# Score tile ahead of the max tile in the first pair of each attention slot, on TensorE's queue

## The chip, the cores and the metric

The kernel runs on one core of a Trainium2 chip (trn2). The metric is the device time of one execution in microseconds (us). Engines are called PE (TensorE), PEld (its weight loads), DVE (VectorE), ACT (ScalarE), POOL (GpSimd) and SP (SyncE, which here only issues DMAs).

## The reference

The input is x, 8 sequences of 1024 tokens with 256 features. Three blocks follow one another:

```python
x = x + 0.5 * ffn(layernorm(x))      # top-2 gated expert + shared projection
x = x + attention(layernorm(x))      # 16 heads of 16 dims, causal
x = x + 0.5 * ffn(layernorm(x))
```

The change is in the attention:

```python
q = q / math.sqrt(D)
scores = jnp.einsum('bhqd,bhkd->bhqk', q, k)
scores = jnp.where(causal, scores, -inf)
attn = jax.nn.softmax(scores, axis=-1)
out = jnp.einsum('bhqk,bhkd->bhqd', attn, v)
```

The softmax subtracts each query's maximum over its keys before the exponential.

## The kernel before

There are three stages, one after the other: `stage_a` (first feed-forward block and the projections to q, k and v, in 16 chunks of 512 tokens), `stage_b` (attention) and `stage_c` (output projection and second feed-forward block). Each engine's program is written out by hand, in order, with semaphores between the engines; there is no scheduler.

`stage_b` works through 32 groups of four heads (8 sequences x 16 heads). The scores of a group are computed twice.

- The first time ("max tiles") only the row maxima are wanted. `max_tile` (L1157) gives PE a tile of one PSUM bank (queries on the partitions, up to 512 keys along the bank; one matmul or two), and two tiles make a unit. DVE reads a unit out of a pair of banks (`maximum`, L1094; `dve_unit`, L435): one custom instruction for each of one or two reductions, each with a read of the accumulator into `pm`. The last read of a unit raises `m_read`. There are two pairs of banks, so the first tile of a unit waits until DVE has read the unit two before it (L1162). There are 36 max tiles, 18 units, to a group.
- The second time ("score tiles") the scores come transposed, keys on the partitions. `score_tile` (L1165) multiplies k with q; two more rows of the operands carry the maximum, negated, so that it is subtracted by the matmul. ACT takes the exponential of the tile into `b_probs` (L1079). Score tiles have three PSUM banks in a ring, so a tile waits until ACT has read the tile three before it (`p_ready`, L1182). POOL zeroes the blocks above the diagonal.

A group's score tiles are divided into nine slots of four heads (`SLOTS`; the causal triangle is packed in rows of 512 columns, so that a slot's tile is one matmul of 512 columns in slots 0 and 3 to 7, and two matmuls in slot 1 (384 + 128), 2 (256 + 256) and 8 (384 + 128)). After the third tile of each slot comes the value step of two slots before (`values`, L1188; col-tiled matmuls of `b_probs` with v). So PE goes through nine slots of four pairs each, a pair being a max tile of one or two groups ahead and a score tile of this group. The order in which this stands on PE's queue is the loop at L1224 to L1231, and nothing else sets it. The first group's maxima are computed ahead, and the last group has no max tiles between its score tiles.

The max tile of the first pair has an odd number in its group, so it completes a unit: it is the one that DVE waits for. The max tile of the second pair opens the next unit and waits for DVE. The third completes, the fourth opens.

Which half of the operands' rows a head has depends on its number (`head_rows`): even heads lie from row 0, odd ones from row 64. The heads of the score tiles are taken in the order 1, 0, 2, 3 (`S_ORDER`), and the max tiles beside them have the other half each time.

Once a group, in slot 6 after the value step, PE transposes the negated maxima of the next group (`turn_m`, L1154), ACT copies them (L1058), and a DMA puts them into the rows of q for the score tiles of that group, from slot 0 on.

Of the kernel before, what the change touches and what calls it, by code (L numbers as in the profile page):

```python
# [116 lines left out]
def head_rows(h, n):  # L117

    return slice(h % 2 * HALF, h % 2 * HALF + n)
# [741 lines left out]
def stage_b(nc, psum, pairs_of_banks, const, scratch, ahead, chunk):  # L861
    ident, _, zero, *_, hold = const
    with ExitStack() as ctx:
# [65 lines left out]
        def score_bank(g, t, last):  # L929

            if last:
                n = t % (SB + MB)
                return m_bank[n - SB] if n >= SB else s_bank[ring(g, n) % SB]
            return s_bank[ring(g, t) % SB]

        def turn_bank(g):

            return s_bank[(ring(g, TURN_TILE) - 1) % SB]

        def groups(eng, step):  # L940

            step(Group(0, 0), False)
            with loop(eng, 0, (NG - 2) // NBUF) as r:
                for k in range(1, NBUF + 1):
                    step(Group(r, k), False)
            step(Group(0, NG - 1), True)
# [196 lines left out]
        @block.tensor  # L1143
        def _(pe):
            def turn_m(g):

                pe.wait_ge(m_chain, g.at(2, 2))
                if g.k or not isinstance(g.r, int):
                    p = g.next(-1)
                    pe.wait_ge(p_ready, p.at(TILES, TURN_TILE - SB + 1))  # L1150
                    bank = turn_bank(p)
                else:
                    bank = s_bank[SB - 1]
                pe.transpose(bank[:, 0:P],  # L1154
                             mparts[:].rearrange("p q r n -> p (q r n)").bitcast(F32), ident[:]).then_inc(m_turned, 1)

            def max_tile(g, t):  # L1157
                u = t // 2
                if t == 0:
                    pe.wait_ge(stacked[g.buf], g.turn(STACK, STACK))  # L1160
                if t % 2 == 0 and not (g.first and u < 2):
                    pe.wait_ge(m_read, g.at(NUNIT, u - 1))  # L1162
                ahead.pe_unit_tile(pe, qs[g.buf], ks[g.buf], u, t % 2, m_bank[t % MB])

            def score_tile(g, s, n, last):  # L1165
                t, h = s * GH + n, S_ORDER[n]
                if t == 0:
                    if g.first:
                        pe.wait_ge(ones_placed, 16 * 2 * NBUF)
                    pe.wait_ge(m_placed[g.buf], g.turn(32, 32))  # L1170
                if last and t >= SB:
                    if t == SB:
                        pe.wait_ge(m_read, NG * NUNIT + UNITS_AHEAD)
                    if t >= SB + MB:
                        pe.wait_ge(p_ready, g.at(TILES, t - SB - MB + 1))
                elif not last and TURN_TILE <= t < TURN_TILE + SB:
                    if t == TURN_TILE + SB - 1:
                        pe.wait_ge(m_out, g.at(1, 2))
                    else:
                        pe.wait_ge(p_ready, g.at(TILES, t - SB + 2))  # L1180
                elif not (g.first and t < SB):
                    pe.wait_ge(p_ready, g.at(TILES, t - SB + 1))  # L1182
                for j, q0, w, off in SLOTS[s]:
                    done = pe.matmul(score_bank(g, t, last)[:, off:off + w], ks[g.buf][head_rows(h, SROWS_M), h // 2, j * P:(j + 1) * P],  # L1184
                                     qs[g.buf][head_rows(h, SROWS_M), h // 2, q0:q0 + w], start=True, stop=True)
                done.then_inc(s_tile, 1)

            def values(g, s):  # L1188

                pe.wait_ge(p_ready, g.at(TILES, GH * (s + 1)))  # L1190
                if DIAG[s]:
                    pe.wait_ge(p_masked, g.at(ND, DIAG_SLOTS.index(s) + 1))
                if s == 0:
                    pe.wait_ge(vx_ready, g.at(1, 1))
                    if not g.first:
                        pe.wait_ge(o_out, g.at(2))
                if s == LOW_DONE + 1:
                    pe.wait_ge(o_out, g.at(2, 1))
                pieces = VALUE_PIECES[s]
                for n, (src, j, q0, w, off) in enumerate(pieces):  # L1200
                    col = q0 % BANK
                    for h in range(GH):
                        last = pe.matmul(o_bank[2 * D * h:2 * D * (h + 1), col:col + w], vx[g.buf][:, j, h, :],  # L1203
                                         probs[:, PROB_BUF[src], h, off:off + w], start=(j == 0),
                                         stop=(s in (LOW_DONE, HIGH_DONE) and n == len(pieces) - 1),
                                         tile_position=(0, 2 * D * h))
                last.then_inc(pv_done, 1)

            def event(g, s):
                if s >= 2:  # L1210
                    values(g, s - 2)
                elif not g.first:
                    values(g.next(-1), NSLOT - 2 + s)

            def step(g, last):
                def maxima(s, n):
                    if not last:
                        t = (s + AHEAD) * GH + n + 1
                        if t < TILES:
                            max_tile(g.next(1), t)  # L1220
                        else:
                            max_tile(g.next(2), t - TILES)

                for s in range(NSLOT):  # L1224
                    for n in range(GH):
                        maxima(s, n)
                        score_tile(g, s, n, last)
                        if n == GH - 2:
                            event(g, s)
                            if s == TURN_SLOT and not last:  # L1230
                                turn_m(g.next(1))  # L1231

            for t in range(2 * UNITS_IN_A, TILES):
                max_tile(Group(0, 0), t)
            for t in range(AHEAD * GH + 1):
                max_tile(Group(0, 1), t)
                if t == GH - 1:
                    turn_m(Group(0, 0))
            groups(pe, step)
            for s in (NSLOT - 2, NSLOT - 1):  # L1240
                values(Group(0, NG - 1), s)
# [453 lines left out]
```

## Time and profile before

| what | value |
|---|---|
| median of 3 runs | 1322.26 us (1321.27 to 1323.11) |
| the profiled execution, its own time | 1320.54 us |
| its span, first to last instruction | 1318.7 us |
| PE matmul busy, share of the span | 1225.8 us, 93% |
| PE weight loads | 801.9 us, 61% |
| DVE | 1105.0 us, 84% |
| ACT | 921.7 us, 70% |
| POOL | 434.7 us, 33% |
| granted clock of TensorE, mean | 0.971 |
| DVE, the reductions of the max tiles (L435), 1036 of them | 727.1 us, mean 753 ns |
| ACT, the exponentials (L1079), 1152 of them | 598.6 us, mean 609 ns |

The busy time of an engine is the union of its instructions' times; PE's matmuls are pipelined and their ends are modelled, so a busy PE needn't be at its peak. In the page's picture of the span in 40 slices, slices 12 to 33 (the attention) have PE, DVE and the granted clock at 9 tenths or more throughout.

### The profile page before, as it was taken

How to read it: one execution, taken by the hardware profiler on the slowest of the kernel's cores; microseconds unless marked ns; L12 is line 12 of the kernel's file. 1: busy time of each engine (PE TensorE's matmuls, PEld its weight loads, DVE VectorE, ACT ScalarE, POOL GpSimd, SP SyncE). 2: the span in 40 equal slices, each digit the busy share in tenths (PEclk: the TensorE clock that was granted, in tenths of full speed). 3: DMA queues.
4: the chain of work that ended last, by engine and by line, in shares of the span. 5: the costliest groups of instructions: out<-in, count | busy, mean ns of one | idle time of the engine just before them, and what ended most of it. 6: DMA issues, size and time to landing. Idle time of an engine off the chain costs nothing. (4 is left out here: it accounts for less than half of the span.)

```text
span 1318.7 us, 35998 instructions
## 1 busy us (share of the span) xinstructions
PE 1225.8 (93%) x9331; PEld 801.9 (61%) x9331; DVE 1105.0 (84%) x3904; ACT 921.7 (70%) x1858; POOL 434.7 (33%) x843
## 2 busy tenths in 40 slices
PE   3999999997999999999999999999999996799996
PEld 3988888875544444444444444444444442799996
DVE  4788888868999999999999999999999994567775
ACT  3666666641777887887887887887887887356663
POOL 3333333301222222222322322322222222577771
PEclk9999999997899999999999999999999999799998
DMA  3356655893464654664664644654654643556641
GB/s 116 129 222 223 223 223 223 244 266 100 72 108 83 107 102 82 108 101 82 108 101 82 113 96 85 109 96 86 109 96 89 112 89 111 192 171 197 203 149 65
DMA packets 121853, 173.74 MB, mean 132 GB/s; under 512 B 44012, under 2 KB 71788, under 8 KB 121804
## 3 DMA queue, kind: packets, MB, share of 16 engines
q1 hardware_dynamic: 121816, 173.30, 54.4%
q8 instruction: 17, 0.28, 0.1%
q14 instruction: 20, 0.16, 0.0%
HBM read 96.08 MB, written 76.02 MB: 131 GB/s over the span
## 5 line engine op out<-in xcount | busy, mean ns | idle before, releaser
L435 DVE CUSTOM_DVE_ANT_0 junk<-banks,mask 128x768 bf16<-128x768 f32 (+7 forms) x1036 | 727.1, 753 | 6.0 <-issue 5.7
L1079 ACT ACTIVATE b_probs<-banks 128x512 f32<-128x512 f32 x1152 | 598.6, 609 | 135.6 <-PE banks L1184 131.3
L428 PE MATMUL banks<-ks,qs 48*128 48x512 f32 (+3 forms) x1056 | 295.5, 386 | 24.4 <-DVE pm L435 15.7
L1203 PE MATMUL banks<-b_probs,b_vx 128*32 128x512 f32 (+3 forms) x3072 | 308.2, 496 | 4.3 <-POOL b_probs L1039 2.0
L1184 PE MATMUL banks<-qs,ks 50*128 50x512 f32 (+3 forms) x1056 | 309.2, 389 | 0.8 <-ACT b_probs L1079 0.4
L428 PEld LDWEIGHTS banks<-ks,qs 48*128 48x128 f32 x1056 | 168.9, 191 | 184.3 <-DVE pm L435 153.6
L165 POOL TENSOR_TENSOR hold_pool<-zero 128x1 f32<-128x1 f32 x192 | 37.2, 194 | 592.6 <-ACT b_probs L1079 463.5
L1184 PEld LDWEIGHTS banks<-qs,ks 50*128 50x128 f32 x1056 | 164.9, 187 | 21.5 <-ACT b_probs L1079 18.4
L1039 POOL TENSOR_SCALAR_AFFINE_SELECT b_probs<-b_probs 128x512 f32<-128x512 f32 x256 | 158.3, 636 | 0.0
L428 PE MATMUL banks<-b_ks,b_qs 48*128 48x512 f32 (+2 forms) x499 | 135.9, 376 | 7.6 <-DVE pm L435 6.2
L1184 PE MATMUL banks<-b_qs,b_ks 50*128 50x512 f32 (+2 forms) x480 | 142.2, 386 | 0.2
L1203 PEld LDWEIGHTS banks<-b_probs,b_vx 128*32 128x32 f32 x3072 | 70.6, 108 | 109.3 <-issue 81.1
L428 PEld LDWEIGHTS banks<-b_ks,b_qs 48*128 48x128 f32 x499 | 77.1, 184 | 81.5 <-DVE pm L435 67.5
L172 PE MATMUL banks<-wh,a_ln_xh 128*128 128x256 f32 (+1 forms) x384 | 113.8, 296 | 5.8 <-DVE a_ln_xl L279 5.8
L172 PE MATMUL banks<-wh,a_ln_xl 128*128 128x256 f32 (+1 forms) x384 | 110.5, 288 | 0.0
L172 PE MATMUL banks<-wl,a_ln_xh 128*128 128x256 f32 (+1 forms) x384 | 110.2, 287 | 0.0
L257 ACT ACTIVATE a_ln_xn<-a_x,a_ln_nbias,a_ln_rstd 128x256 f32<-128x256 f32 x128 | 72.3, 592 | 22.0 <-POOL a_ln_nbias L249 21.6
L435 DVE DVE_READ_ACCUMULATOR2_ANT pm<- 128x1 f32 x1036 | 86.1, 83 | 0.0
L172 PEld LDWEIGHTS banks<-wh,a_ln_xh 128*128 128x128 f32 x384 | 74.6, 194 | 10.3 <-issue 5.0
L162 DVE MEMSET hold_dve<- 128x1 f32 x662 | 39.1, 59 | 48.8 <-PE banks L428 33.5
L1184 PEld LDWEIGHTS banks<-b_qs,b_ks 50*128 50x128 f32 x480 | 75.6, 184 | 6.7 <-ACT b_probs L1079 6.0
L172 PEld LDWEIGHTS banks<-wl,a_ln_xh 128*128 128x128 f32 x384 | 74.7, 195 | 0.8
(118 smaller groups left out, 1945.3 us busy)
## 6 DMA issues: line engine op xcount, KB each, us to landing
scr_qk<-a_qk SPq DMA_DIRECT2D x64, 512.0 KB, 3.0
qs<-scr_qk SPq DMA_DIRECT2D x132, 128.0 KB, 4.4
ks<-scr_qk SPq DMA_DIRECT2D x132, 128.0 KB, 4.9
scr_o<-b_o SPq DMA_DIRECT2D x64, 256.0 KB, 2.3
b_qs<-scr_qk SPq DMA_DIRECT2D x66, 128.0 KB, 3.7
b_ks<-scr_qk SPq DMA_DIRECT2D x66, 128.0 KB, 3.9
a_x<-x SPq DMA_DIRECT2D x16, 512.0 KB, 3.4
scr_x<-a_x SPq DMA_DIRECT2D x16, 512.0 KB, 2.7
```

Source lines behind the costliest of these rows:

```text
L162: dve.memset(self.dve_out[:, col:col + 1], 0.0)
L165: pool.tensor_tensor(self.pool_out[:, col:col + 1], zero[:, 0:1], zero[:, 1:2], ALU.add)
L172: last = pe.matmul(out, a, b, start=(n == 0), stop=(n == len(terms) - 1))
L257: act.activation(self.xn[:, t, :], x[:, t, :], ACT.Identity, scale=self.rstd[:, t:t + 1], bias=self.nbias[:, t:t + 1]).then_inc(self.xn_re ...
L428: last = pe.matmul(bank[:, off:off + w], qs[head_rows(h, SROWS), h // 2, i * P:(i + 1) * P], ks[head_rows(h, SROWS), h // 2, k0:k0 + w], s ...
L435: ins = dve.tensor_tensor_reduce(self.junk[:, u % 2, off:off + w], pair[:, off:off + w], self.mask[:, 2 * BANK - w:2 * BANK], 1.0, 0.0, AL ...
L1039: ins = pool.affine_select(out=blk, in_=blk, compare_op=ALU.is_ge, fill=0.0, base=0, pattern=[[0, GH], [1, P]], channel_multiplier=-1)
L1079: act.activation(probs[:, PROB_BUF[s], h, :], score_bank(g, t, last)[:], ACT.Exp).then_inc(p_ready, 1)
L1184: done = pe.matmul(score_bank(g, t, last)[:, off:off + w], ks[g.buf][head_rows(h, SROWS_M), h // 2, j * P:(j + 1) * P], qs[g.buf][head_row ...
L1203: last = pe.matmul(o_bank[2 * D * h:2 * D * (h + 1), col:col + w], vx[g.buf][:, j, h, :], probs[:, PROB_BUF[src], h, off:off + w], start=( ...
```

## The change

In each slot, the first of the four pairs is issued with the score tile first and the max tile second. The other three pairs stay as they are. No instruction is added or taken away.

```diff
                 for s in range(NSLOT):
                     for n in range(GH):
-                        maxima(s, n)
-                        score_tile(g, s, n, last)
+                        if n == 0:
+                            score_tile(g, s, n, last)
+                            maxima(s, n)
+                        else:
+                            maxima(s, n)
+                            score_tile(g, s, n, last)
                         if n == GH - 2:
                             event(g, s)
```

On PE's queue, from the last pair of slot 7 to the second pair of slot 8, before. L428 are max tiles, L1184 score tiles; numbers behind a name are buffers, and `m_read` and `b_p_ready` are the waits for DVE and ACT:

```order
L428 MATMUL banks2<-b_ks2,b_qs2 128x512 [waits m_read]
L1184 MATMUL banks1<-qs0,ks0 128x512 [waits b_p_ready]
L428 MATMUL banks2<-b_ks2,b_qs2 128x128
L428 MATMUL banks2<-b_ks2,b_qs2 128x384
L1184 MATMUL banks0<-qs0,ks0 128x384 [waits b_p_ready]
L1184 MATMUL banks0<-qs0,ks0 128x128
L428 MATMUL banks3<-b_ks2,b_qs2 128x512 [waits m_read]
```

The same place in the changed kernel:

```order
L428 MATMUL banks2<-b_ks2,b_qs2 128x512 [waits m_read]
L1184 MATMUL banks1<-qs0,ks0 128x512 [waits b_p_ready]
L1184 MATMUL banks0<-qs0,ks0 128x384 [waits b_p_ready]
L1184 MATMUL banks0<-qs0,ks0 128x128
L428 MATMUL banks2<-b_ks2,b_qs2 128x128
L428 MATMUL banks2<-b_ks2,b_qs2 128x384
L428 MATMUL banks3<-b_ks2,b_qs2 128x512 [waits m_read]
```

The two pieces of the score tile have moved ahead of the two of the max tile; both score tiles are now neighbours, and so are the two max tiles behind them.

The same queue from the last pair of slot 4 to the third pair of slot 5, where every tile is one matmul, before:

```order
L428 MATMUL banks2<-ks1,qs1 128x512 [waits m_read]
L1184 MATMUL banks0<-qs0,ks0 128x512 [waits b_p_ready]
L428 MATMUL banks2<-ks1,qs1 128x512
L1184 MATMUL banks1<-qs0,ks0 128x512 [waits b_p_ready]
L428 MATMUL banks3<-ks1,qs1 128x512 [waits m_read]
L1184 MATMUL banks0<-qs0,ks0 128x512 [waits b_p_ready]
```

And in the changed kernel:

```order
L428 MATMUL banks2<-ks1,qs1 128x512 [waits m_read]
L1184 MATMUL banks0<-qs0,ks0 128x512 [waits b_p_ready]
L1184 MATMUL banks1<-qs0,ks0 128x512 [waits b_p_ready]
L428 MATMUL banks2<-ks1,qs1 128x512
L428 MATMUL banks3<-ks1,qs1 128x512 [waits m_read]
L1184 MATMUL banks0<-qs0,ks0 128x512 [waits b_p_ready]
```

The max tile that completes a unit (the one without a wait) now stands behind a score tile that waits for ACT.

## Rows read from the trace of the kernel before

**Rows 1.** Waits of PEld and DVE, 400 to 1100 us: total, times, longest

```profile
PEld banks L428 <- DVE pm L435: 191.7, 357, 0.8
DVE hold_dve L162 <- PE banks L428: 31.3, 131, 0.4
```

**Rows 2.** Line 1154, 400 to 1100 us

```profile
L1154 PE MATMUL banks<-ident,b_mparts x28: 327/328/331, 422.4 to 1086.9; 128*128 128x128 f32 x28
```

**Rows 3.** Timeline of PE, slots 8 and 0: start, duration, line, operation

```profile
523.82 0.49 PE L428 MATMUL banks<-ks,qs 48*128 48x512 f32 x1
...
524.16 0.22 PE L428 MATMUL banks<-ks,qs 48*128 48x128 f32 x1
524.16 0.33 PE L1184 MATMUL banks<-qs,ks 50*128 50x384 f32 x1
524.22 0.39 PE L428 MATMUL banks<-ks,qs 48*128 48x384 f32 x1
524.34 0.22 PE L1184 MATMUL banks<-qs,ks 50*128 50x128 f32 x1
...
526.51 0.50 PE L428 MATMUL banks<-ks,qs 48*128 48x512 f32 x1
...
528.17 1.06 PE L1203 MATMUL banks<-b_probs,b_vx 128*32 128x512 f32 x8
529.16 0.49 PE L428 MATMUL banks<-ks,qs 48*128 48x512 f32 x1
```

**Rows 4.** Timeline of DVE, same slots

```profile
524.58 0.08 DVE L435 DVE_READ_ACCUMULATOR2_ANT pm<- 128x1 f32 x1
...
524.81 0.82 DVE L435 CUSTOM_DVE_ANT_0 junk<-banks,mask 128x640 bf16<-128x640 f32 x1
...
527.27 0.08 DVE L435 DVE_READ_ACCUMULATOR2_ANT pm<- 128x1 f32 x1
```

**Rows 5.** Timeline of PEld, slot 0

```profile
527.41 0.18 PEld L428 LDWEIGHTS banks<-ks,qs 48*128 48x128 f32 x1 [0.37 <-DVE pm L435]
```

**Rows 6.** Timeline of PE, slot 3 of the group before

```profile
510.09 0.50 PE L428 MATMUL banks<-b_ks,b_qs 48*128 48x512 f32 x1
...
510.84 0.50 PE L428 MATMUL banks<-b_ks,b_qs 48*128 48x512 f32 x1
...
511.75 0.53 PE L1203 MATMUL banks<-b_probs,b_vx 128*32 128x384 f32 x4
```

**Rows 7.** Timeline of ACT, slot 3 of the group before

```profile
510.66 2.06 ACT L1079 ACTIVATE b_probs<-banks 128x512 f32<-128x512 f32 x4 [0.58 <-PE banks L1184]
```

**Rows 8.** Timeline of PE, slot 1

```profile
529.50 0.33 PE L428 MATMUL banks<-ks,qs 48*128 48x384 f32 x1
...
529.67 0.22 PE L428 MATMUL banks<-ks,qs 48*128 48x128 f32 x1
...
530.09 0.49 PE L428 MATMUL banks<-ks,qs 48*128 48x512 f32 x1 [0.20 <-DVE pm L435]
...
530.89 1.07 PE L1203 MATMUL banks<-b_probs,b_vx 128*32 128x384 f32 x16
```

**Rows 9.** Timeline of PE, slot 2

```profile
532.24 0.33 PE L1184 MATMUL banks<-b_qs,b_ks 50*128 50x256 f32 x1
...
532.41 0.28 PE L1184 MATMUL banks<-b_qs,b_ks 50*128 50x256 f32 x1
532.69 0.50 PE L428 MATMUL banks<-ks,qs 48*128 48x512 f32 x1
...
533.68 1.06 PE L1203 MATMUL banks<-b_probs,b_vx 128*32 128x512 f32 x8
```

**Rows 10.** Timeline of DVE, slot 1

```profile
530.10 1.09 DVE L435 CUSTOM_DVE_ANT_0 junk<-banks,mask 128x896 bf16<-128x896 f32 x1
```

**Rows 11.** Timelines of PE and DVE, slot 5 of the group before

```profile
515.31 0.39 PE L428 MATMUL banks<-b_ks,b_qs 48*128 48x512 f32 x1
...
515.99 0.69 DVE L435 CUSTOM_DVE_ANT_0 junk<-banks,mask 128x512 bf16<-128x512 f32 x1
```

## Prediction

> Names first. PE issues, in each slot, four pairs: M0 to M3 are the max tiles of a later group, S0 to S3 the score tiles; V is the value step, which stands between pair 2 and pair 3. "M1(3)" is M1 of slot 3. I follow a slot from its predecessor's M3 and S3, the first work after a value step, over pairs 0, 1 and 2 to its own V.
>
> **What bounds the kernel now.** The page says that PE and DVE are both busy for nine tenths of the middle stage, so the share of neither decides; I read next who waits for whom there. PE waits 191.7 us for DVE's reads of the max banks; DVE waits 31.3 us for PE, in 131 places of the listed size [rows 1]. So the two wait for each other. The transposes of the running maxima, one a group, give the pace: 28 of them from 422.4 to 1086.9, 24.61 us a group [rows 2]. Then I read one group in order of time, for the hand-over that comes last in each slot.
>
> DVE side. In slot 8, M0 is two matmuls, 128 columns at 524.16 and 384 at 524.22, which ends at 524.61 [rows 3]. DVE's previous unit was read out at 524.58 and the next could have followed it at once, as odd units do; it starts at 524.81, 0.20 after M0's end [rows 4]. M0 thus sets DVE's start. DVE then works through two units; the last read-out, at 527.27, releases the weights of M1(0) at 527.41 [rows 4, 5], and V(0) comes at 528.17, 0.76 after it [rows 3]. So there is a path M0(8), DVE, M1(0), V(0), M3(1), in which every step waits for the one before.
>
> ACT side. In slot 3, M3 and S3 start at 510.09, ACT, idle for 0.58, starts on S3 at 510.66, S2 waits for that exp to leave its bank, and V follows at 511.75: 1.66 after M3 [rows 6, 7]. M1(3) was there at 510.84, and 0.76 after it would be 511.60. Here ACT sets V, with 0.15 to spare for DVE. So each slot has a floor of 1.66 from M3 to V, and only a slot that sits above its floor is led by M1, that is by an M0 of the slot before. V(0) at 528.17 is 1.66 after M3(0) at 526.51 [rows 3]: both at once. V(1) is at 530.89, 1.73 after M3(1), and 0.80 after M1(1) (its score tiles have two pieces) [rows 3, 8]: led by DVE.
>
> **The change, part by part.** Nothing is added or removed; in nine places a group, S0 goes ahead of M0 in PE's queue, S3 and S0 become neighbours, and so do M0 and M1. The waits move along: M0 has none of its own and now stands behind S0's wait for an exp. That exp is the one of three tiles earlier and long done: M0 and S0 start at the same 524.16 now [rows 3]. At slot 0, S0 also waits for the maxima, which a DMA places after slot 6's transpose; two whole slots lie between, so I cost that at nothing. On SP, POOL, ACT and DVE no instruction moves.
>
> *Where S0 is one matmul* (slots 0, 3 to 7). M and S use opposite halves of the rows and run side by side, so M0, issued second, starts about 0.01 later than now. Costs: 0.01 where M0 leads the next V.
>
> *Where S0 is two matmuls* (slots 1, 2, 8). The second piece needs the half that the first one holds: S0(8) has its pieces at 524.16 and 524.34, 0.18 apart [rows 3]. Everything behind it starts no earlier. That PE starts its matmuls in order is seen in slot 2: the second piece of S0, queued behind M0's pieces of 384 and 128 columns, starts at 532.41, 0.17 after its own first piece (532.24), although 256 columns take only about two thirds of the 0.17 that 384 take (M0(1): 529.50 to 529.67) [rows 8, 9]. So M0 would be late by 0.18 in slot 8, 0.17 in slot 1 and, with 256 columns ahead, 0.12 in slot 2. The Trainium skill (TensorE: Matmul & The Clock Gate, Part 3, The mechanism) says that matmuls are in order in start and end; the row agrees.
>
> Now through the group, each shift against the same slot of now.
> 1. M0(8) +0.18. DVE was waiting for it, so DVE starts +0.18, M1(0) +0.18, V(0) +0.17 (it was at its floor and at DVE's time together).
> 2. V(1): M3(1) is 0.17 late, M1(1) only 0.01, since M0(0) is one of the cheap ones. By the ACT floor (1.66, and 0.02 for the two pieces) V(1) comes at 529.16 + 0.17 + 1.68 = 531.01 instead of 530.89: +0.12. So 0.05 is given back.
> 3. M0(1) is late by 0.17 from M3(1) and 0.17 of its own, 0.34. DVE started on it at 530.10, 0.21 after its end at 529.89 (529.67 + 0.22), so it had no reserve [rows 8, 10]. M1(2), 532.69 now, comes at 533.03; with 0.80 to V, V(2) is at 533.83 instead of 533.68 [rows 9] (now set by ACT, which has an output to copy first): +0.15.
> 4. M0(2) is 0.12 late of its own, M1(3) 0.24 in all, against M3(3) +0.15: 0.09 of the 0.15 to spare is used, nothing goes on.
> 5. Slots 3 to 7 repeat slot 3's picture or have DVE still busy: at slot 5 M0 starts at 515.31 and ends at 515.70, DVE takes the unit at 515.99 [rows 11], and the 0.09 by which S0(5) trails there fits in. The 0.01 of M0(4) and M0(7) passes on: +0.02.
>
> Sum: 0.18 - 0.01 - 0.05 + 0.03 + 0.02 = 0.17 us a group. 31 of the 32 groups have max tiles between their score tiles: 31 x 0.17 = 5.3 us. The profiled execution (1318.7 span, 1320.5 with what lies around it) would become 1325.8; the runs' median lies 1.7 above it, at 1322.3, and becomes **1327.6**.
>
> What the trace doesn't show is the price of two neighbours on one half. Bounds: nothing (M0(1)'s pieces of 384 and 128 columns are such neighbours and follow each other after 0.17 [rows 8], the streaming time) up to 0.11, the part of the 0.34 from M3(8) at 523.82 to M0(8) at 524.16 [rows 3] that isn't streaming (512 columns at the rate of 384 in 0.17 are 0.23). I take nothing, since the neighbours' row is the same case. Also, at each third group's step from slot 8 to 0 the loop's back edge falls in front of S0, with at most 0.2 us for M0 ten times, of which slot 1's reserve takes most: 0 to 2 us, taken as 0.
>
> **Rivals.**
> A. The weights of S0 aren't loaded while S3 streams, so S0, and M0 behind it, come 0.11 later in every slot. For it: the visible 0.11 after each value step. Against: the neighbouring pieces. It passes where DVE leads the next V (M0 of 8, 4 and 7): 3 x 0.11 + 0.17 = 0.50 a group, 15.5 us: 1337.8. The Trainium skill (the same page, Part 3) has a weight load overlap running matmuls only on another row group, which would make this the case; but M3 and M0, on one half too, are now loaded 0.1 apart and M0 follows with no second load seen.
> B. M0 doesn't wait for S0's second piece, or DVE has more reserve at slot 8 than 0.20 between end and start suggests. Then only the lags of 0.01 are left: 0.02 to 0.05 a group, 1 us: 1323.3. For it: ends of matmuls are modelled. Against: slot 2's row.
> C. Faster. S0(2) gets its second piece at 532.36 instead of 532.41, and in the groups at the loop edge S0(0) goes ahead of its counting instructions. If ACT ever waited for S0, that would be 0.05 x 31, some 1.6 us: 1320.7. It decides only where exp finds no S0; but ACT runs four exps on end once S3 is there, 2.06 us without a gap [rows 7], and S0 has a whole exp of reserve.
> That the change does nothing is excluded by the order of the built program.
>
> **How the numbers follow.** Forecast (slower, by 3 to 9 us) 0.62, A 0.10, B 0.22, C 0.06. A measurement of this kernel tells 0.2%, 2.6 us, from no change, so slower 0.72, same 0.22, faster 0.06. The range takes in B and the forecast with its loop-edge bound and half of A's price: 1322.8 to 1335; left out are C and most of A.
>
> **What would show it.** The transposes would be 24.78 apart. Slots 8 and 1 would have M0's first piece at the time of S0's second, 0.51 after M3 instead of 0.34, and DVE's start after M0's end still 0.20. M3 to M3 would grow by 0.17 from slot 0 to 1, shrink by 0.05 in the next and stay within 0.03 elsewhere. DVE's waits for PE would rise from 31.3 by some 5 us or more, ACT's waits for PE by as much; busy times stay. M3 to M0 gaps over 0.4 in one-piece slots would speak for A, an unchanged 24.61 for B; the forecast is wrong if V(1) isn't pulled back to its floor (more than 0.17) or if slot 0 has reserve that I took as none.

## The result and the profile after

The changed kernel is slower: 1324.79 us median of 20 runs (1319.66 to 1331.30) against 1321.84 us for the kernel before in as many runs beside it (1318.53 to 1328.34). The ratio on record is 1.0030, with a 95% interval of 1.0019 to 1.0041: between 2.5 and 5.4 us, against a forecast of 5.3. (The ratios in this document aren't those of the medians; that would be 1.0022 here.) The forecast time was 1327.6; the median lies 2.8 below it and 1.5 above rival B's 1323.3, so the time alone doesn't tell which of the two had the mechanism. Two executions among those below, 1847.67 us in the kernel with slot 8 alone and 1698.73 us in the one with the change on top of unit signals, were far slower than the rest, and the ratios leave them out.

The profiled execution has a span of 1320.7 us, only 2.0 above that of before, because its attention began earlier: the first transpose is at 319.9 instead of 322.2. From the first to the last of the 32 it takes 769.1 us instead of 764.7. DVE's and ACT's busy times hardly changed (DVE 1105.6 us against 1105.0, ACT 924.0 against 921.7), so what was added is waiting.

The waits of PEld and DVE between 400 and 1100 us in the changed kernel (total, times, longest), the rows of [rows 1]:

```profile
PEld banks L428 <- DVE pm L435: 198.6, 355, 0.8
DVE hold_dve L162 <- PE banks L428: 37.1, 140, 0.4
```

DVE waits 5.8 us longer for max tiles. And the pace, the row of [rows 2] (line 1154 in the same stretch; what counts are the first and the last start):

```profile
L1154 PE MATMUL banks<-ident,b_mparts x28: 327/328/331, 420.6 to 1089.0; 128*128 128x128 f32 x28
```

27 groups in 668.4 us are 24.76 us a group, where it was 24.61. That is 0.145 us a group, 4.5 us over 31 groups: all of the difference (3.9 us by the ratio), and close to the 0.17 of the forecast. But it isn't lost where the forecast had put it. The start of slot 8 on PE, which answers to [rows 3] (start, duration, line and operation):

```profile
522.68 0.50 PE L428 MATMUL banks<-ks,qs 48*128 48x512 f32 x1
...
523.02 0.22 PE L428 MATMUL banks<-ks,qs 48*128 48x128 f32 x1
523.02 0.34 PE L1184 MATMUL banks<-qs,ks 50*128 50x384 f32 x1
523.08 0.39 PE L428 MATMUL banks<-ks,qs 48*128 48x384 f32 x1
523.20 0.22 PE L1184 MATMUL banks<-qs,ks 50*128 50x128 f32 x1
```

In the queue both pieces of S0 (L1184) stand ahead of both pieces of M0 (L428). On the array M0's pieces start at 523.02 and 523.08, 0.34 and 0.40 after M3, exactly as before, and ahead of S0's second piece at 523.20. So here a matmul on one half of the rows started without waiting for one ahead of it in the queue on the other half. DVE in the same slot, the second row of [rows 4]:

```profile
523.67 0.82 DVE L435 CUSTOM_DVE_ANT_0 junk<-banks,mask 128x640 bf16<-128x640 f32 x1
```

M0 ends at 523.47, DVE starts 0.20 later, as before. Slot 8 costs nothing. Now slots 1 and 2, where S0 has two pieces too (PE, the rows of [rows 8] and [rows 9]):

```profile
528.57 0.22 PE L1184 MATMUL banks<-b_qs,b_ks 50*128 50x128 f32 x1
528.58 0.22 PE L428 MATMUL banks<-ks,qs 48*128 48x128 f32 x1
...
531.17 0.33 PE L1184 MATMUL banks<-b_qs,b_ks 50*128 50x256 f32 x1
531.34 0.22 PE L428 MATMUL banks<-ks,qs 48*128 48x128 f32 x1
531.34 0.28 PE L1184 MATMUL banks<-b_qs,b_ks 50*128 50x256 f32 x1
```

and DVE's starts on the units that these M0 complete:

```profile
529.04 1.09 DVE L435 CUSTOM_DVE_ANT_0 junk<-banks,mask 128x896 bf16<-128x896 f32 x1
...
531.87 1.09 DVE L435 CUSTOM_DVE_ANT_0 junk<-banks,mask 128x896 bf16<-128x896 f32 x1
```

In slot 1 M0 and S0 both end at 528.80, within 0.01 (start and duration added), and DVE starts 0.24 later, where it was 0.21 [rows 8, 10]. In slot 2 M0 ends at 531.55 and S0 at 531.62; DVE starts 0.31 after M0, 0.25 after S0. It looks as if DVE learns of M0 only once S0, ahead of it in the queue, has ended too and has been signalled. Taken over all groups of the two traces (the start of DVE's custom row less start and duration of M0's last row; medians in ns; a slot counts from the M3 with which it begins, as in the prediction, and the last column compares the time from this M3 to the next one):

| slot | DVE start after M0's end, before | after | S0's end against M0's end, after | M3 to next M3, after less before |
|---|---|---|---|---|
| 0 | 207 | 246 | 4 earlier | 0 |
| 1 | 206 | 251 | 2 later | +47 |
| 2 | 206 | 312 | 63 later | 0 |
| 3 | 207 | 244 | 4 later | -3 |
| 4 | 207 | 245 | 3 later | +36 |
| 5 | 293 | 325 | 84 later | +2 |
| 6 | 206 | 245 | 4 earlier | +2 |
| 7 | 206 | 252 | 2 later | -4 |
| 8 | 206 | 207 | 49 earlier | +51 |

The trace also records when each semaphore was raised, and there the reading can be seen. M0's signal comes 14 to 15 ns after M0's end in the kernel before. In the changed kernel it comes at 52 to 59 ns, in slot 2 at 119 and in slot 5 at 133, each time 34 to 43 ns behind S0's signal; only in slot 8, where S0's signal is 50 ns ahead, is it at 15 still. DVE starts 192 or 193 ns after M0's signal in both kernels (in slot 5 before the change it is busy until later). The same thing happens to S0 in the kernel before: in slot 8 it ends 49 ns ahead of M0, which stands ahead of it in the queue, and its signal comes 106 ns after its end, behind M0's.

The last column says where that delay ends up: +47 in slot 1 (led by M0 of slot 0), +36 in slot 4 and +51 in slot 8 (led by M0 of slot 7), 134 ns in all. In slot 4 the value step is short, and M3 itself waits for DVE's read of the slot's own unit. At the loop's back edge, one group in three, S0 of slot 0 starts late: before, 0.55 after M3, with M0 at 0.34. Now M0 stands behind it, and both start at 0.39 to 0.40. It is the only place where M0's start is late, by 0.06, and there the successive transposes grow by 0.18 instead of 0.12 to 0.13 (24.84 against 24.66; the others 24.71 against 24.58): 0.02 more a group on average.

This gives theory L: the halves start on their own; completions are reported in the queue's order; and a signal costs a few hundredths of a microsecond of those behind it. Theory R is the one on record: matmuls start in the queue's order, and M0 starts late.

### The profile page after: what moved, and what is told of

The parts are those of the page before. It is cut to its first block and busy times, and to the rows that moved or that the text cites. A ratio compares the mean times of both kernels' runs of the same rounds, so it can differ in the third digit from the quotient of the medians.

```text
span 1320.7 us, 35988 instructions
## 1 busy us (share of the span) xinstructions
PE 1216.6 (92%) x9331; PEld 794.3 (60%) x9331; DVE 1105.6 (84%) x3904; ACT 924.0 (70%) x1858; POOL 434.8 (33%) x843
## 5 line engine op out<-in xcount | busy, mean ns | idle before, releaser
L428 PE MATMUL banks<-ks,qs 48*128 48x512 f32 (+3 forms) x1056 | 294.5, 385 | 28.1 <-DVE pm L435 19.4
L1184 PE MATMUL banks<-qs,ks 50*128 50x512 f32 (+3 forms) x1056 | 305.4, 389 | 0.9 <-ACT b_probs L1079 0.4
L428 PEld LDWEIGHTS banks<-ks,qs 48*128 48x128 f32 x1056 | 169.5, 190 | 188.6 <-DVE pm L435 159.1
L1184 PEld LDWEIGHTS banks<-qs,ks 50*128 50x128 f32 x1056 | 164.4, 187 | 19.3 <-ACT b_probs L1079 14.0
L428 PE MATMUL banks<-b_ks,b_qs 48*128 48x512 f32 (+2 forms) x499 | 135.6, 376 | 10.7 <-DVE pm L435 8.5
L1184 PE MATMUL banks<-b_qs,b_ks 50*128 50x512 f32 (+2 forms) x480 | 141.0, 386 | 0.2
L428 PEld LDWEIGHTS banks<-b_ks,b_qs 48*128 48x128 f32 x499 | 77.7, 184 | 84.9 <-DVE pm L435 71.0
L1184 PEld LDWEIGHTS banks<-b_qs,b_ks 50*128 50x128 f32 x480 | 75.4, 184 | 5.2 <-ACT b_probs L1079 4.0
```

The source lines that it names most:

```text
L428: last = pe.matmul(bank[:, off:off + w], qs[head_rows(h, SROWS), h // 2, i * P:(i + 1) * P], ks[head_rows(h, SROWS), h // 2, k0:k0 + w], s ...
```

## The experiments

All are the kernel before with one edit, or with two of them together where the text says so. Times are against the kernel before, run beside them: its median is 1321.42 us beside the first four kernels, 1322.24 beside the two that move S0's signal and beside the last of all, 1321.27 beside the others. The pace is that of line 1154 (1155 where the edit adds a line above it), from the row as above.

### Which slots carry it

Three kernels take the change apart by slots:

```diff
-                        maxima(s, n)
-                        score_tile(g, s, n, last)
+                        first, second = (score_tile, maxima) if n == 0 and s == 8 else (maxima, score_tile)
+                        for f in (first, second):
+                            f(s, n) if f is maxima else f(g, s, n, last)
```

The second has `n == 0 and s in (0, 4, 7)` there, the third `n == 0 and s in (1, 2, 3, 5, 6)`.

Slot 8 alone.

> Only slot 8 has S0 ahead of M0. Theory R (the one on record: matmuls start in the queue's order, so M0 of slot 8 is late by the 0.18 us of S0's second piece, which leads DVE, M1(0) and V(0)): M0(8) at 0.51 after M3, about +0.12 us a group, 3 to 4 us slower (ratio 1.003). Theory L (from the trace of the changed kernel: the halves start on their own, only the signal of M0 waits for S0's signal and comes about 0.04 after it; in slot 8 M0 ends 0.05 after S0 anyway): M0(8) still at 0.34, DVE 0.21 after M0's end, transposes 24.61 apart, no change (ratio 1.000).

Measured: 1320.31 us, ratio 1.0004 (0.9982 to 1.0026).

```profile
L1154 PE MATMUL banks<-ident,b_mparts x28: 327/328/331, 422.4 to 1086.8; 128*128 128x128 f32 x28
```

24.61 us a group. M0's median start stays 0.337 after M3, DVE's 0.206 after M0's end. The main term of the forecast is zero.

Slots 0, 4 and 7.

> Only slots 0, 4 and 7 have S0 ahead of M0; these are the slots whose M0 leads the next slot. Theory R: starts late by 0.01 each, 0.03 us a group, under 1 us in all (ratio 1.0007). Theory L: DVE starts 0.245 instead of 0.206 after M0's end in these three, each passes on: 0.12 to 0.13 us a group, nearly the whole of the change's 0.145; 4 us slower (ratio 1.003).

Measured: 1325.49 us, ratio 1.0035 (1.0020 to 1.0049).

```profile
L1154 PE MATMUL banks<-ident,b_mparts x28: 327/328/329, 420.6 to 1089.0; 128*128 128x128 f32 x28
```

24.76 us, the same as the whole change. DVE starts 245, 244 and 251 ns after M0's end in these slots and 206 in the others, except for slot 5, which DVE reaches late. The three slots carry everything.

The other five.

> Slots 1, 2, 3, 5 and 6 have S0 ahead of M0: the slots whose M0 doesn't lead, with two-piece tiles in 1 and 2. Theory L: DVE's start after M0's end is 0.25 in slot 1 and 0.31 in slot 2, but the next V is led by ACT there; 0 to 0.02 us a group, no change (ratio 1.000). Theory R without slot 8: M0(1) +0.17 and M0(2) +0.12, absorbed too; ratio 1.000. A third theory, that any delay of DVE's start costs its time, wants about 0.27 us a group, 8 us (ratio 1.006).

Measured: 1321.51 us, ratio 0.9996 (0.9966 to 1.0026).

24.60 us a group (423.4 to 1087.7). DVE does start late here, 250 ns after M0's end in slot 1 and 310 in slot 2, and nothing comes of it: M1(3) is 0.10 later against M3, and V(3) stays at 1.65, where ACT has it. So the slots' leaders had been read rightly: M0 of these five slots leads nothing, at delays of this size.

### Is it the place in the queue, or the signal?

The fourth pair, where it is ACT that waits.

```diff
-                        maxima(s, n)
-                        score_tile(g, s, n, last)
+                        first, second = (score_tile, maxima) if n == 3 and s < 8 else (maxima, score_tile)
+                        for f in (first, second):
+                            f(s, n) if f is maxima else f(g, s, n, last)
```

Slot 8 keeps its order.

> The order of before, but the fourth pair is turned instead of the first: S3 ahead of M3 in slots 0 to 7 (slot 8 keeps its order). Here ACT waits for S3 after the value step. Theory L: M3's signal no longer stands ahead of S3's, so ACT starts 0.04 sooner in the slots after 0 to 7, and where ACT leads V (slots 3, 4, 6, 7 and 2) the slot is 0.04 shorter; where M1 leads nothing moves at once, though a slot may become led by M1: 0.05 to 0.2 us a group faster, 2 to 6 us (ratio 0.996 to 0.999). Theory R (no price on signals, starts 0.004 apart): no change, ratio 1.000.

Measured: 1317.84 us, ratio 0.9978 (0.9963 to 0.9992), faster. PE and ACT in slot 3 of one group:

```profile
506.63 0.50 PE L428 MATMUL banks<-b_ks,b_qs 48*128 48x512 f32 x1
...
508.24 0.53 PE L1203 MATMUL banks<-b_probs,b_vx 128*32 128x384 f32 x4
```

```profile
507.16 1.57 ACT L1079 ACTIVATE b_probs<-banks 128x512 f32<-128x512 f32 x3 [0.54 <-PE banks L1184]
```

ACT starts on S3 0.53 after M3 began, 0.57 in [rows 6, 7]; V follows M3 by 1.61 instead of 1.66. The pace is 24.53 (419.2 to 1081.5), 0.08 a group faster, 2.5 us. Slots 3, 6 and 7 are each about 0.04 shorter; slot 8, which M1 leads, is 0.04 longer, and slots 2 and 4, which had been named too, are as long as before. What S0 does to M0 in the change, M3 did to S3 all along: S3's signal comes 14 ns after its end here, where it was at 44 to 49 (slot 5 aside).

Only the second tile of a unit signals DVE; the order is that of before.

```diff
-        last.then_inc(self.m_tile, 1)
+        if half == 1:
+            last.then_inc(self.m_tile, 1)
...
-                dve.wait_ge(m_tile, g.at(TILES, 2 * u + 2))
+                dve.wait_ge(m_tile, g.at(NUNIT, u + 1))
```

> The order of before, but only the second tile of a unit signals DVE (DVE waits for units, not tiles), so M1 and M3 signal nobody. It parts two readings of theory L. L1: what costs is a signal ahead in the line, 0.04 us each. Then S3's signal comes 0.04 sooner without any change of order, ACT-led slots are 0.04 shorter as in the run with pair 3 turned: transposes 24.53 apart instead of 24.61, 2 to 3 us faster (ratio 0.998). L2: what costs is standing second in the queue. Then nothing changes, ratio 1.000.

Measured: 1320.68 us, ratio 1.0005 (0.9989 to 1.0020).

```profile
L1155 PE MATMUL banks<-ident,b_mparts x28: 327/328/330, 422.0 to 1085.0; 128*128 128x128 f32 x28
```

24.56 us, between L1 and L2 by the pace: S2, which waits for the exp of S3, starts 1.193 after M3 in slots 4, 6 and 7 instead of 1.218, so the signal ahead was worth 0.025, not 0.04. The stage wins 1.7 us by the pace, which would be a ratio of 0.9987. The times don't show it; their interval begins just above, at 0.9989.

The change on top of unit signals.

> Unit signals with the change itself (S0 ahead of M0 in all slots). Theory L1: M0's signal still waits for S0's, so against unit signals alone it costs the change's 0.13 to 0.15 us a group again: transposes about 24.67 apart, 2 us slower than before (ratio 1.001 to 1.002). Rival: the price came from four signals close together, two of them from M3 and S3; with M3's gone M0's is in time and the ratio is that of unit signals alone, 0.998.

Measured: 1326.53 us, ratio 1.0042 (1.0026 to 1.0058).

24.69 us a group (423.0 to 1089.7), 0.14 above unit signals alone. DVE's start is 245 ns after M0's end in slots 0, 3 and 6 again: M3's signal had no part in it. (Against the kernel before the pace explains 2.5 us, and the ratio gives 5.6, at the least 3.4; the profiled execution, the fastest of the five, has a span 2.1 us above that of before. The runs don't say where the rest comes from.)

Then the 0.04 was divided: slots 0, 4 and 7 turned as in the second kernel, but S0 signals nobody, and S1 raises ACT's count by two. The control has the late signal without the turned pairs.

```diff
-                done.then_inc(s_tile, 1)
+                late = s in (0, 4, 7) and not last
+                if not (late and n == 0):
+                    done.then_inc(s_tile, 2 if late and n == 1 else 1)
```

> As the run with slots 0, 4 and 7 turned, but S0 of these slots signals nobody; S1 raises the count by two for both (ACT takes S0's exp some 0.4 us later, which its idle time covers). It divides the 0.04 us: if it is the price of S0's signal in the line (0.026 by the run with unit signals), DVE starts 0.21 to 0.22 after M0's end instead of 0.245, and 0.02 to 0.05 us a group are left of 0.13: transposes 24.63 to 24.66 apart, ratio 1.000 to 1.001. If it is the order of completion alone, with no price on the signal, DVE's start stays at 0.245, the transposes 24.74 apart, ratio 1.003.

> Control for the last: the order of before, with the late signal of S0 in slots 0, 4 and 7 alone. ACT's exp of S0 comes later there and the ones behind it close up. If ACT's idle time covers it, the transposes are 24.61 apart and the ratio 1.000; DVE's start 0.206 after M0's end. If it isn't covered, up to 0.4 us in each of the three slots, 1.2 us a group, ratio 1.02, and the run beside it has to be read against this one.

Measured: 1335.12 us (ratio 1.0101, 1.0062 to 1.0139) and, for the control, 1331.38 us (1.0069, 1.0045 to 1.0093). The expectation that ACT's idle time covers the late signal was wrong, and both kernels are slower than the change itself: in slot 5 ACT's copy and exps close up, V(5) comes at 2.24 after M3 instead of 1.89, and the pace is 24.96 (422.1 to 1096.0). So the time of the first kernel says nothing by itself, but the two can be read against each other. Slot 4 with S0 unsignalled, PE and DVE:

```profile
514.17 0.39 PE L428 MATMUL banks<-b_ks,b_qs 48*128 48x512 f32 x1
514.17 0.39 PE L1184 MATMUL banks<-qs,ks 50*128 50x512 f32 x1
```

```profile
514.78 1.22 DVE L435 CUSTOM_DVE_ANT_0 junk<-banks,mask 128x1024 bf16<-128x1024 f32 x1
```

DVE starts 0.22 after M0's end at 514.56. The medians in slots 0, 4 and 7 are 221, 220 and 225 ns; with the order of before 207, with the signal 245, 244 and 251. So of the 0.04 about 0.025 is S0's signal and 0.015 the order of completion. The pace is 25.03 (422.1 to 1097.8), 0.07 above the control, half of the change's price. Most of this half lies at the loop's back edge, where M0 starts late as well: there the transposes are 25.15 apart against 25.00, in the other groups 24.96 against 24.94. Away from the edge, then, only 0.02 of the change's 0.12 to 0.13 is left without S0's signal.

### A faster kernel

By the same reading, in the slots led by DVE, S1 and S2 stand behind M1's wait for nothing. So S1 was put ahead of M1 (the same edit with `n == 1`), alone and then with unit signals.

> The order of before, but the second pair turned: S1 ahead of M1, which waits for DVE. The other pairs stay. If the M1-led slots (5, 1, 8) lose time because S1 and S2 queue up behind M1's wait, V follows M1 by about 0.67 instead of 0.75: 0.05 to 0.08 in slots 1 and 5, 0.01 in slot 8, some 0.13 us a group, 4 us faster (ratio 0.997). Rival: V after M1 is bound by M1 and M2 themselves, on one half, and nothing is won (ratio 1.000). No signal that DVE or ACT waits for stands later than before.

Measured: 1317.85 us, ratio 0.9973 (0.9958 to 0.9989), at 24.45 us a group (29 transposes, 404.1 to 1088.8). Slot 1 on PE:

```profile
510.17 0.50 PE L428 MATMUL banks<-b_ks,b_qs 48*128 48x512 f32 x1
...
510.75 0.45 PE L1184 MATMUL banks<-qs,ks 50*128 50x384 f32 x2
511.21 0.49 PE L428 MATMUL banks<-b_ks,b_qs 48*128 48x512 f32 x1
...
511.87 1.07 PE L1203 MATMUL banks<-b_probs,b_vx 128*32 128x384 f32 x16
```

Both pieces of S1 (510.75) now run while M1 still waits, and V follows M1 by 0.66, where it was 0.80 [rows 8]. Over all groups the median in slot 1 is 0.71, since there V meets its floor. By the medians slots 1, 8 and 5 are shorter by 0.09, 0.04 and 0.03. Part of it comes from V standing 1.65 after M3 in slots 1 and 8, with no allowance for their two-piece tiles: there S1 used to be on the path. The rival, that M1 and M2 themselves bound V, is excluded.

The profiled execution is the slowest of the twelve (1323.18 us), and not for the pace: from 338 to 353 us, in the first group, the granted clock is 0.50 (1.2 GHz) where the kernel before has 0.99. PE had been busy for 20.7 of the 26 us before that stretch, against 22.0, at a granted clock of 0.51 and 0.50. The first two transposes are 30.6 us apart instead of 26.5.

Now with unit signals as well.

> Both of the last two: unit signals, and S1 ahead of M1. If both act, DVE-led and ACT-led slots get shorter together and neither catches the gain of the other: more than the sum, 0.25 to 0.35 us a group, 8 to 11 us faster (ratio 0.992 to 0.994). If pair 1 gives nothing, it is the unit signals' 0.998.

Measured: 1311.20 us, ratio 0.9942 (0.9923 to 0.9961).

24.33 us a group (419.6 to 1076.5), 0.28 a group faster: more than 0.16 and 0.06 apart.

And with the fourth pair turned too, in slots 0 to 7.

> The fastest so far (unit signals, pair 1 turned, 24.33 us a group) with the fourth pair turned too in slots 0 to 7. By the signal's price M3 has none left to hold S3 up with, and what turning pair 3 still gives is the difference of the two runs, 0.04 - 0.026 = 0.014 in each of the five ACT-led slots: 0.05 to 0.07 us a group more, transposes 24.27 apart, ratio about 0.992 against 0.994. If the unit signals have taken all that turning gives, 24.33 and 0.994.

Measured: 1311.07 us, ratio 0.9905 (0.9868 to 0.9941).

```profile
L1155 PE MATMUL banks<-ident,b_mparts x28: 327/328/331, 422.0 to 1077.7; 128*128 128x128 f32 x28
```

24.29 us, 0.04 more. Between this and the last the times don't decide (the intervals overlap, the medians are 0.1 us apart); both beat the kernel before, by 8 and 13 us by their ratios.

## Why the prediction was right, and where it wasn't

- **What bounds the kernel**: right. The two loops, DVE-led through M0 and M1 and ACT-led through S3 and S2, and the rule that only what exceeds a slot's floor counts, gave the right answer in all three kernels that split the change: a delay of 0.04 passed whole in slots 0, 4 and 7, and one of 0.10 in slot 2 not at all. Whether M0(8) leads V(0), the first step of the walk, stays untested: no run delayed it.
- **"Where S0 is two matmuls"**: wrong, and with it points 1 and 3 of the walk through the group. M0(8) was to be 0.18 late and is on time; M0(1) and M0(2) too. The step that failed is "PE starts its matmuls in order is seen in slot 2". In the changed kernel S0(2) has the same 0.17 between its pieces (531.17 and 531.34) though nothing of M0 stands between them any more, and M0 starts ahead of S0's second piece in slot 8. That row had another reason, which I had not looked for. One that fits is the load of the second piece's weights: in slot 2 it starts 0.05 after the first piece, in slots 1 and 8 together with it (medians of both kernels), and max tiles of 256 and 256 columns follow each other after 0.12. No run tried it.
- **"Where S0 is one matmul ... about 0.01 later"**: the place was right, the size wrong. M0's start isn't late, except by 0.06 at the loop's back edge; its signal is, by 0.04. The point that counted only 0.02 in the sum is nearly the whole of it: three slots, 0.13 us. That M0(4) acts on M3 at the end of its own slot, and not on V(5), was missed; the price is the same.
- **The loop's back edge**: a bound of 0 to 2 us, taken as 0; measured 0.02 a group, 0.6 us.
- **The sum**: 0.17 us a group against 0.145 measured, from other terms: 0.18 that is nothing, minus 0.05 that has nothing to give back, and 0.02 that is 0.13. The 0.03 of slot 2 is nothing too. The near agreement is luck. The sign isn't: every theory in which M0 waits for something of S0 has it.
- **The signs named in advance**: transposes at 24.78 (24.76) and DVE's waits up by some 5 us (5.8) held. The second is no evidence: DVE's waits went up by 11.3 us (to 42.6) with slots 0, 4 and 7 turned, at the same price, and down by 5.3 (to 26.0) with the other five. M0 at 0.51 after M3 in slots 8 and 1 and DVE's start still 0.20 after M0's end (it is 0.25 in slot 1) both failed, and these two are what separates R from L. M3 to M3 failed as well: 0.17 more in slot 0 and 0.05 less in slot 1 were named, and it is 0 and 0.05 more, with 0.04 and 0.05 more in slots 4 and 8. By the forecast's own words it is wrong if V(1) isn't pulled back to its floor, and V(1) moved away from it, from 1.74 to 1.79 after M3. ACT's waits for PE were to rise as much as DVE's and hardly moved (112.6 to 113.2 us among the listed).
- **Rivals**: A (a visible weight load, 0.11 each) is excluded: M0 starts at 0.34 everywhere but at the back edge. B had the premise right, M0 doesn't wait for the second piece, and its sum wrong, 1 us where the ratio's interval begins at 2.5, since it left only the lag in the start. C is excluded by the pace.

## What to carry to other kernels

When two matmuls run side by side, look at when the waiting engine starts after the end of the one it needs, and not at the matmul's start alone: the one it needs should be first in the queue, and matmuls in front of it should signal nobody who doesn't need it. Order each pair by who leads: the tile that DVE waits for first where DVE leads, the tile that ACT waits for first where ACT leads, and nothing that could run behind a wait it doesn't share. A row that fits a rule (here, in-order starts) shows it only if the same row would look different without the rule.

## What the runs showed of the hardware that I had not expected

Matmuls on opposite halves of the rows can start out of the queue's order: M0's pieces, third and fourth in the queue, started at 523.02 and 523.08, the second piece of S0 ahead of them at 523.20. Their completions reach the other engines in order: with S0 ending 63 ns after M0 by the profile's modelled ends (slot 2), DVE started 312 ns after M0's end instead of 206. The Trainium skill (TensorE: Matmul & The Clock Gate, Part 3, The mechanism) has both starts and ends in order; the trace agrees for the completions as they are signalled, and not for the starts. A signal ahead costs about 25 ns (S2 at 1.193 instead of 1.218 after M3 without M3's signal; 245 to 220 ns at DVE without S0's). The Trainium skill (the same page, Part 3, The cost: per-tile semaphore tail) puts an increment at 26.3 ns; the trace agrees.
